# Decoder layer stack on one core: keys turned ahead of the feed-forward matmuls, keys' projection in halves, norms of queries and keys apart

## What is computed

```python
def attn_layer(x, Wqkv, qs, ksc, Wo):      # 16 heads of 64
    q, k, v = split(x @ Wqkv)              # x with half of its channels one token later
    q = l2norm(q) * qs; k = l2norm(k) * ksc            # t / max(|t|, 1e-12), per head
    q = q * cos * scale + rotate_half(q) * sin * scale
    k = k * cos / scale + rotate_half(k) * sin / scale
    # windows of 32 queries see the 32 keys before them and their own 32
    out = softmax(mask(8 * q k^T)) v
    return out @ Wo
def ffn_layer(x, g, bln, W1, b1, W2, b2):  # hidden width 341, value and gate
    xn = (x - mean) / sqrt(var + 1e-5) * g + bln
    a, gate = split(xn @ W1 + b1)
    return a * gelu(gate) @ W2 + b2
# per layer: x = x + attn_layer(x); x = x + ffn_layer(shift(x))
```

## Time and profile before

| | |
|---|---|
| median of 3 runs | 2223.14 us (2221.44 to 2223.32) |
| profiled execution: time, span | 2225.41 us, 2223.6 us |
| PE busy | 2016.6 us, 91% of the span |
| weight loads busy | 1195.3 us, 54% |
| DVE busy | 1359.7 us, 61% |
| ACT busy | 1357.9 us, 61% |
| POOL busy | 1079.4 us, 49% |
| granted TensorE clock, mean | 0.984 |

### The profile page before, as it was taken

The page is one execution under the profiler, slowest core; times in us unless marked ns, Lnnn a source line. Parts: engine busy times, 40 slices in busy tenths (PEclk is TensorE's granted clock), DMA queues, the critical chain, the costliest instruction groups (busy, mean ns, idle before and its releaser), DMA issues.

```text
span 2223.6 us, 73529 instructions
## 1 busy us (share of the span) xinstructions
PE 2016.6 (91%) x32616; PEld 1195.3 (54%) x32616; DVE 1359.7 (61%) x1663; ACT 1357.9 (61%) x1669; POOL 1079.4 (49%) x708
## 2 busy tenths in 40 slices
PE   8999997789999999999999999999999999999987
PEld 5655654355555555555555555555555555555553
DVE  1454454666666666666667666666666676667662
ACT  5556553456666666666666666666666666666664
POOL 0000000576555655565556555655555556556640
PEclk9999997799999999999999999999999999999999
DMA  3000000122223222232222322222322223222220
GB/s 105 1 1 1 1 20 29 39 59 59 59 60 86 68 68 59 59 89 69 67 59 69 86 59 76 72 57 69 78 70 68 59 59 88 68 69 59 59 59 19
DMA packets 82055, 128.02 MB, mean 58 GB/s; under 512 B 17230, under 2 KB 28108, under 8 KB 81740
## 3 DMA queue, kind: packets, MB, share of 16 engines
q1 hardware_dynamic: 81740, 123.33, 21.4%
HBM read 21.55 MB, written 1.05 MB: 10 GB/s over the span
## 4 chain that ended last, share of the span: by engine, by line
PE 64%; ACT 16%; issue 8%; DVE 7%; POOL 4%; DMA 0%; POOLq 0%; ACTq 0%; SPq 0%; DVEq 0%
PE ps L609 14%; PE ps L613 8%; PE ps L635 7%; PE ps L673 5%; PE ps L690 5%; PE ps L666 5%; ACT KT L990 4%; PE ps L422 3%; PE ps L653 3%; PE ps L618 2%; PE ps L622 2%; POOL work L1405 2%; DVE work L1083 2%; DVE work L1080 2%; ACT ps L981 2%
## 5 line engine op out<-in xcount | busy, mean ns | idle before, releaser
L1405 POOL TENSOR_TENSOR work<-work,RS 128x1024 f32<-128x1024 f32 x192 | 361.6, 1904 | 312.4 <-ACT RS L1024 312.4
L613 PEld LDWEIGHTS ps<-ident,work 128*128 128x128 f32 x3072 | 346.8, 142 | 150.6 <-issue 71.0
L1080 DVE TENSOR_TENSOR work<-ps,work 128x1024 f32<-128x1024 f32 x192 | 230.7, 1202 | 314.3 <-ACT work L1003 303.0
L613 PE MATMUL ps<-ident,work 128*128 128x128 f32 x3072 | 396.6, 277 | 27.9 <-POOL work L1405 12.5
L1399 POOL TENSOR_TENSOR work<-work 128x1024 f32<-128x1024 f32 x96 | 226.2, 2356 | 372.8 <-DVE work L1083 372.8
L609 PE MATMUL ps<-WK,XS 128*128 128x512 f32 x384 | 190.8, 620 | 50.0 <-ACT KT L990 49.8
L1083 DVE TENSOR_TENSOR work<-ps,work 128x1024 f32<-128x1024 f32 x192 | 233.0, 1214 | 0.0
L1119 DVE TENSOR_REDUCE SS<-work 128x16 f32<-128x1024 f32 x192 | 232.0, 1209 | 0.0
L1392 POOL TENSOR_TENSOR work<-work 128x1024 f32<-128x1024 f32 x96 | 226.1, 2356 | 5.7 <-DVE work L1083 5.7
L950 ACT ACTIVATE work<-ps 128x1024 f32<-128x1024 f32 x96 | 98.1, 1022 | 210.0 <-PE ps L673 208.2
L673 PEld LDWEIGHTS ps<-work 64*32 64x32 f32 x12288 | 135.4, 105 | 165.4 <-issue 109.2
(11 more groups left out here) (183 smaller groups left out, 3097.8 us busy)
## 6 DMA issues: line engine op xcount, KB each, us to landing
work<-work SPq DMA_DIRECT2D x576, 128.0 KB
work<-work SPq DMA_DIRECT2D x336, 64.0 KB
WQ<-in_wqkv SPq DMA_DIRECT2D x6, 512.0 KB, 3.6
WK<-in_wqkv SPq DMA_DIRECT2D x6, 512.0 KB, 4.0
WV<-in_wqkv SPq DMA_DIRECT2D x6, 512.0 KB, 3.7
WO<-in_wo SPq DMA_DIRECT2D x6, 512.0 KB, 3.9
work<-ZR SPq DMA_DIRECT2D x48, 64.0 KB
W<-in_w SPq DMA_DIRECT2D x6, 341.0 KB, 3.0
```

Of the source, the lines that this page charges most:

```text
L613: m = nc.tensor.transpose(flat(R)[:, t * 128:t * 128 + 128], src[:, t * 128:t * 128 + 128], ident[:, :])
L1080: V.tensor_tensor(h16(cos_part[:, j, :]), h16(flat(src)), rotary_tabs[:, at:at + 64].unsqueeze(1).broadcast_to([PARTS, 16, 64]), ALU.mult) ...
L1405: U.tensor_tensor(h16(qk_norm[:, j, :]), h16(cos_part[:, j, :]), inv_norms[:, j, :].unsqueeze(2).broadcast_to([PARTS, 16, 64]), ALU.mult). ...
```

## The change

- TensorE: the heads are turned ahead of the values. The keys are turned right behind the values, ahead of the feed-forward's part, and are signalled in two halves. The keys' projection waits for and signals each half alone. `hid(1)` stands whole ahead of the weighing, the last chunk's gate between its halves, its value matmul behind it. Gates are signalled alone (`gates_ready`).
- ScalarE: the copy of the heads goes ahead of that of the values. The copy of the turned keys and the squares of the keys come in halves of 512 columns. The GELU table is loaded between the copies of keys and queries. The inverse norms come in a pair for the queries and a pair for the keys (`invert_norms`); the queries' pair stands ahead of the squares of the keys, but in steps n = 1 it is put off to the next step, behind the copy of the heads. `ffn_affine` goes. `copy_heads` stands ahead of the keys' norms and of `inverse` at n = 0, and behind the keys' norms at n = 2 and 3.
- VectorE: the rotation of the keys in four instructions of 512 columns. Clamps apart for queries and keys, each a maximum over pairs whose second member is 1e-24, set once by GpSimd. `gated(1)` stands behind maximum and difference of the scores. `norm` gets a second instruction in place of `ffn_affine`.
- GpSimd: the queries' product with the inverse norms comes ahead of the keys' rotation, in steps n = 1 behind the keys' product.

```diff
@@ TensorE, step
                     project(bank_z, w_q, 1, n).then_inc(q_projected, 1)
+                if d:
+                    pe.wait_ge(heads_copied, g - 2)
+                    turn(bank_y, heads).then_inc(heads_turned, 1)
...
                     m.then_inc(values_ready, 1)
-                if d:
-                    pe.wait_ge(heads_copied, g - 2)
-                    turn(bank_y, heads).then_inc(heads_turned, 1)
+                if b:
+                    pe.wait_ge(k_normed, g)
+                    if d:
+                        pe.wait_ge(heads_turned_copied, g - 2)
+                    turn(bank_y, qk_norm[:, 1, :], 0, 4).then_inc(k_turned, 1)
+                    turn(bank_y, qk_norm[:, 1, :], 4, 8).then_inc(k_turned, 1)
...
-                    pe.wait_ge(k_normed, g)
-                    if d:
-                        pe.wait_ge(heads_turned_copied, g - 2)
-                    turn(bank_y, qk_norm[:, 1, :]).then_inc(k_turned, 1)
...
-                    if due(g):
-                        pe.wait_ge(k_turned_copied, g)
-                    project(bank_y, w_k, 0, n)
-                    project(bank_y, w_k, 1, n).then_inc(k_projected, 1)
+                    for half in range(2):
+                        if due(g):
+                            pe.wait_ge(k_turned_copied, 2 * g - 1 + half)
+                        project(bank_y, w_k, half, n).then_inc(k_projected, 1)
...
                     pe.wait_ge(hidden_gated, 3 * f + 1)
-                    hid_gate(1, bank_f)
+                    hid(1, bank_f)
...
-                    hid_value(1, bank_f)
+                    pe.wait_ge(gate_gelu, 3 * f + 2)
+                    hid_gate(2, bank_f)
...
                     pe.wait_ge(hidden_gated, 3 * f + 2)
-                    hid(2, bank_f)
+                    hid_value(2, bank_f)
@@ ScalarE
+            def invert_norms(g, j):
+                clamped, logs, inverse_done, normed_ = ((q_clamped, q_norms_log, q_inverse, q_normed), (k_clamped, k_norms_log, k_inverse, k_normed))[j]
+                act.wait_ge(clamped, g + 1)
+                A(norm_logs[:, 16 * j:16 * j + 16], sq_clamped[:, 16 * j:16 * j + 16], ACT.Ln).then_inc(logs, 1)
+                act.wait_ge(logs, g + 1)
+                if due(g):
+                    act.wait_ge(normed_, g)
+                A(inv_norms[:, j, :], norm_logs[:, 16 * j:16 * j + 16], ACT.Exp, scale=-0.5).then_inc(inverse_done, 1)
...
+                if n == 2 and f is not None and g - 1 < ALL_BLOCKS:
+                    invert_norms(g - 1, 0)
...
+                elif a:
+                    invert_norms(g, 0)
@@ VectorE
+                V.tensor_reduce(sq_clamped[:, 16 * j:16 * j + 16], sq_sums[:, j, :, :], AX, ALU.max).then_inc(clamped, 1)
...
-                V.tensor_tensor(normed[:, :], bank_f[:, 1, :], spread[:, :], ALU.mult).then_inc(ffn_normed, 1)
+                V.scalar_tensor_tensor(out=bank_f[:, 0, :], in0=bank_f[:, 1, :], scalar=layer_vecs[:, f // 4 * 9 + 6:f // 4 * 9 + 7], in1=spread[:, :], op0=ALU.mult, op1=ALU.mult).then_inc(ffn_normed, 1)
+                dve.wait_ge(ffn_normed, f + 1)
+                V.tensor_scalar(ffn_in[:, :], bank_f[:, 0, :], layer_vecs[:, f // 4 * 9 + 7:f // 4 * 9 + 8], None, ALU.add).then_inc(ffn_input, 1)
@@ GpSimd, step
+                    late = f is not None and n == 1
+                    if not late:
+                        norm_product(g, 0)
...
+                    norm_product(g, 1)
+                    if late:
+                        norm_product(g, 0)
```

More of the change, by code:

```diff
@@ L958, in step @@
                     A(probs[:, :, :, :], scores_sb[:, :, :, :], ACT.Exp).then_inc(probs_exp, 1)
-                if f is not None and n == 1:
-                    ffn_affine(f)
                 if a:
@@ L1351, in _ @@
             cross()
+            dve.wait_ge(zeroed, 7)
             for g in range(ALL_BLOCKS + 3):
```

185 lines of the change are left out of this document (99 added, 86 removed).

## The result

| | before | after |
|---|---|---|
| median, lowest and highest of 20 runs each | 2220.79 us (2216.95 to 2225.25) | 2217.04 us (2209.2 to 2223.66) |
| ratio after to before, 95% interval | | 0.9983 (0.9975 to 0.9991) |
| profiled execution: time, span | 2225.41, 2223.6 us | 2222.9, 2221.1 us |
| granted TensorE clock, mean | 0.984 | 0.983 |

What follows compares the result with a forecast made beforehand. TensorE, busy 91% of the span, was taken as the bound, only its idle time winnable. 25 us from 22 passes plus 6 from early steps, off 2225.4, less 2.3 for the median: 2192 us; range 2157 to 2234 (8 in 10).

Steps and rivals of the forecast that it cites:

- The sum of the steps: Per pass of four steps: 0.5 + 1.1 + 0.8 - 1.25 = 1.15 us gained, times 22 passes: 25 us.
- the section on the bound: TensorE busy 91%, only idle time winnable; four waits named, among them 12.3 us "issue" that no edit addresses.
- Step n = 3: Keys' projection no longer waits for the copied keys, since they are turned three matmuls earlier: gain 0.50 us.
- Step n = 0: Gain 1.1 us: keys' projection 0.75 earlier, weighing 0.35 more by rotating in halves; weighing still waits 0.6.
- Step n = 1: Gain 0.8 us: last chunk no longer waits for the gating; the table load's wait only moves to the keys' turn.
- Step n = 2: Loss 1.25 us: late queries' product on GpSimd delays DVE's sine part, so the queries' turn waits.
- The early steps: 8 steps without feed-forward, bound by a ring of about 16 us: 0.75 us each, so 6 us gained.
- Rival 3: No change: waits only move, "issue" stalls grow from windows' transfers, or keys' turn waits for copied heads each step; 2219, chance 0.12.
- Rival 1: Late queries' product is covered, n = 2 loses nothing: 2.3 us per pass, 2160 us; chance 0.20.
- Rival 2: Slower: some 21 links chained across n = 1 and n = 2 each take longer; at 0.12 more, 2248 us; chance 0.17.
- Rival 4: A drain of 1.28 us behind each table load, in n = 1 and n = 2: 2249 us; chance 0.01.
- The halves on DVE: Price of a 512-column rotation instruction on VectorE: between 0.57 and 0.75 us, taken as 0.61.

Runs made afterwards that it cites:

- after, own buffer: Changed kernel plus a second buffer for the queries' cosine part, so VectorE need not wait for GpSimd's read: 2185.04 us, ratio to before 0.9838.
- keys whole: Changed kernel with the keys squared and rotated again in instructions of 1024 columns, not halves of 512: 2225.2 us, ratio to before 1.0041.
- both undone: Changed kernel with keys turned directly ahead of the queries again and turned keys copied out by one instruction of 1024 columns: 2226.4 us, ratio to before 1.0038.
- experiment 3: Second buffer for the queries' cosine part, added to the changed kernel: 2185.04 us; also with scores and weighing in half as many matmuls: 2095.25 us.
- the two merged kernels: Kernels before and after with scores and weighing in half as many matmuls of 128 columns, heads mixed: before 2164.39 us, after 2124.06 us.
- at 14: Both kernels with 50 filler instructions per pass and 412 start-up waits, blocks beginning 14 instructions behind n = 1's queries' projection: before 2270.3, after 2204.2 us.
- at 152: Both kernels with 50 filler instructions per pass and 136 start-up waits, blocks beginning inside scores and weighing: before 2249.8 us, after 2220.8 us.

## Why the prediction was wrong

**The sum of the steps was right, what it was added to was not.** Undisturbed steps, pauses at the blocks, and the mean pass:

| us per pass | undisturbed | pauses | together | mean pass |
|---|---|---|---|---|
| before | 71.92 | 1.62 | 73.54 | 73.5 |
| after | 70.47 | 3.20 | 73.67 | 73.6 |
| after, own buffer | 69.17 | 2.79 | 71.96 | 71.7 |
| keys whole | 70.92 | 2.60 | 73.52 | 73.7 |
| both undone (keys late, copy whole) | 71.25 | 2.50 | 73.75 | 73.8 |

A pause is counted where two records of PE at a block's beginning are over 0.3 us apart. The step that failed is the one with which the section on the bound ends: "issue" was set down as 12.3 us that no edit addresses, and the sum then held it constant. Only one of its three rows was quoted; together they were 21.8. In its place the runs showed pauses at the blocks of instructions that grew from 1.62 to 3.20 us per pass, 22 x 1.58 = 35 us, when the waits around them shrank and moved. The steps had gained 22 x 1.45 + 7 = 39; 39 - 35 is 4, and 3.8 were measured.

**Step n = 3**, forecast 0.50, measured 0.57. The wait went; the reason given (the early turn) is one of two that suffice, so the number was right and the reason only half shown.

**Step n = 0**, forecast 1.1, measured 1.10. In the step that starts at 1930.94 the projection comes at 7.37 (forecast 7.4) and the weighing 5.15 behind it (5.1), and it still waits 0.60, as forecast. But of the 0.75 at the projection the early turn and the copy in halves are worth 0.27 together (15.42 against 15.15). The rest fits a wait that the forecast had not listed. Before, PE waited for the turned heads to be copied out, ahead of the keys' turn:

```profile
1936.80 1.94 PE L613 MATMUL ps<-ident,work 128*128 128x128 f32 x16 [0.39 <-ACT work L977]
```

With the heads turned ahead of the values this row is gone, also in the run with both parts undone. No run moved that turn alone. The halves are worth 0.41, so the total agrees in part by luck.

**Step n = 1**, forecast 0.8, measured 1.13. The wait for the heads is 1.06 where 1.5 was expected, and the scores begin at 10.94 (853.76 in the step from 842.82) where 11.2 was; this is the 0.3. The gates alone are worth 0.89.

**Step n = 2**, forecast a loss of 1.25, measured 1.36, by the chain as it was told, shown by the second buffer.

**The early steps**, forecast 6, measured 7.2.

**The rivals.** Rival 3 had the time (2219) with a chance of 0.12, and half of its mechanism: the "issue" stalls grew. Its cause, windows' transfers, was wrong, and so was its second half, the keys' turn waiting for the heads in each step: it waits at n = 1 (1.06) and a little at n = 2 (0.4). Rival 1 did not come by itself (n = 2 at 19.51) and was made in experiment 3; its 2.3 per pass should read 2.4, the sum of the three gains. Rival 2 did not come: n = 2 would have had to last over 20.5 and took 19.51. Rival 4 was rightly set aside: the load takes 1.28 and the next instruction of ACT starts 0.01 behind it (716.53, 717.82).

**The halves on DVE.** Four instructions of 512 columns now follow each other in n = 0:

```profile
1940.92 0.69 DVE L1099 TENSOR_TENSOR work<-ps,work 128x512 f32<-128x512 f32 x1 [2.80 <-ACT work L1019]
1941.53 0.68 DVE L1104 TENSOR_TENSOR work<-ps,work 128x512 f32<-128x512 f32 x1
1942.13 0.68 DVE L1099 TENSOR_TENSOR work<-ps,work 128x512 f32<-128x512 f32 x1
1942.72 0.68 DVE L1104 TENSOR_TENSOR work<-ps,work 128x512 f32<-128x512 f32 x1
...
1943.46 0.86 PE L677 MATMUL ps<-work 64*32 64x64 f32 x64 [0.60 <-DVE work L1104]
```

The pitch is 0.60, between the bounds of 0.57 and 0.75 and next to the 0.61 taken.

## What to carry to other kernels

Before summing what a wait is worth, look whether TensorE's "issue" pauses recur at a fixed count of instructions, as they did here at every 256. Here, by theory A, which the runs bore out, a dense stretch of small matmuls was bound by the arrival of its instructions: it used up 256 in 3.0 us, and late blocks came mostly 3.6 to 4.0 us apart. A wait inside it was worth less than its length: of the 39 us that the steps gained 35 came back as pauses. And fewer and larger matmuls paid twice: half as many of them in scores and weighing (with the heads mixed) took 93 us off the changed kernel (2217.0 to 2124.1) and left the change a gain of 40 us and not of 4. Measure steps by their undisturbed length and by their mean: a change that shortens the first and not the second has moved idle time, not removed it. And when two edits can each remove the same wait, undo both before giving the gain to one.

## What the runs showed of the hardware

In the traces of this case the instruction queue's packets went with TensorE's records at 256 to one: 258 packets for 66,127 records in before and in after, 162 for 41,551 in the two merged kernels, 263 for 67,433 at 14 and for 67,295 at 152. Each packet had 16,384 bytes. Where the engine waited for a block in the trace of after, the blocks came mostly 3.6 to 4.0 us apart, although the packet itself was in transfer for only some 1.2 us. Why the next one wasn't brought earlier no run here shows; the pauses ended about 1.4 us after the packet's record.

The waits for semaphores that had long been met were not free on TensorE. In the start-up of the kernel after, where nothing else ran on the engine, 138 more instructions of this kind moved its first matmul from 9.80 (at 152) to 24.81 us (at 14), 0.11 us each. 50 of them spread over a step n = 1, partly beside running matmuls, lengthened it by 1.9 us in the kernel before (20.11 to 22.0) and by 0.3 in the kernel after (18.98 to 19.25), both at 14.

And the place where the blocks of instructions began mattered more than the planned change, which gained 3.8 us: the same kernel after, but for those 138 instructions at the start, took 73.43 us per pass at one place and 71.97 at another, 32 us or 1.4% over 22 passes. So between these two programs a difference of that size came from their count of instructions in the start-up alone.
